# An attention layer with quantised feed-forward: turned rows kept on chip, values moved to the second half, and another order of the weighted sums

## The reference

```python
xn = layernorm(x)                                   # eps 1e-5
q, k, v = (split_heads(xn @ W.T + b) for W, b in ((q_w, q_b), (k_w, k_b), (v_w, v_b)))
attn = softmax(einsum('bhqd,bhkd->bhqk', q / 4, k)) # over all 4096 keys
attention = (attn @ v).reshape(1, 4096, 256) @ out_w.T + out_b
# quant_fp8: scale = min(448 / max|t|, 448), clip(t * scale), round to float8_e4m3
w8, x8 = quant_fp8(weight), quant_fp8(xn)
ffn = bfloat16((x8 @ w8.T) * (x_scale * w_scale) + bias)
out = x + attention + ffn
```

## Time and profile before

| | us |
|---|---|
| median of 3 runs | 1905.43 (1904.55 to 1905.94) |
| profiled execution, its own time | 1905.45 |
| its span | 1903.6 |

### The profile page before, as it was taken

One profiled execution on the slowest core, in us unless ns is written; L12 is line 12 of the kernel. 1 busy time (PEld: TensorE's weight loads), 2 busy tenths in 40 slices (PEclk: granted clock), 3 DMA queues, 4 the chain that ended last, 5 costly groups with the idle time before them and its releaser, 6 DMA issues.

```text
span 1903.6 us, 75615 instructions
## 1 busy us (share of the span) xinstructions
PE 1656.3 (87%) x33482; PEld 564.1 (30%) x33482; DVE 1544.7 (81%) x1974; ACT 1774.4 (93%) x1961; POOL 29.9 (2%) x48
## 2 busy tenths in 40 slices
PE   6978888888888888888888888888888888888888
PEld 4622222222222222222222222222222222222227
DVE  7667888878787887878787887878788887878787
ACT  2359999999999999999999999999999999999991
POOL 0000000000000000000000000000000000000000
PEclk9989999999999999999999999999999999999999
DMA  6640000000010000000010000001000000000002
GB/s 179 205 144 8 23 9 15 21 15 21 7 29 7 16 15 15 21 15 21 7 29 7 11 21 15 21 7 28 7 23 9 15 20 16 21 7 29 7 15 98
DMA packets 62334, 57.12 MB, mean 30 GB/s; under 512 B 20608, under 2 KB 52608, under 8 KB 62016
## 3 DMA queue, kind: packets, MB, share of 16 engines
q1 hardware_dynamic: 62016, 52.36, 9.4%
HBM read 34.74 MB, written 17.30 MB: 27 GB/s over the span
## 4 chain that ended last, share of the span: by engine, by line
ACT 51%; issue 30%; PE 14%; SPq 2%; DVE 1%; ACTq 1%; DMA 0%; DVEq 0%
ACT probs L688 51%; PE banks L1328 5%; PE banks L1297 3%; PE banks L1179 2%; PE banks L1420 1%; PE banks L1190 1%; ACTq L687 1%; DVE o_junk L975 1%; DVE o_sb L974 1%; PE banks L1404 0%; SPq L368 0%; PE banks L1412 0%; PE banks L1163 0%; SPq L371 0%; DMA k_parts<-probs 0%
## 5 line engine op out<-in xcount | busy, mean ns | idle before, releaser
L688 ACT ACTIVATE probs<-banks 128x1024 f32<-128x1024 f32 x1888 | 1731.1, 1193 | 6.7 <-DMA k_parts<-probs 6.2
L1328 PE MATMUL banks<-probs,v_st 64*32 64x512 f32 x15104 | 1004.2, 590 | 2.4
L1297 PE MATMUL banks<-q_st,k_st 50*32 50x512 f16 x16384 | 792.9, 381 | 217.4 <-ACT probs L688 214.2
L1297 PEld LDWEIGHTS banks<-q_st,k_st 50*32 50x32 f16 x16384 | 232.6, 89 | 1151.5 <-ACT probs L688 1093.4
L1008 DVE SCALAR_TENSOR_TENSOR horner<-horner,bits 128x1024 f32<-128x1024 f32 x320 | 393.2, 1229 | 11.0
L1328 PEld LDWEIGHTS banks<-probs,v_st 64*32 64x32 f32 x15104 | 272.0, 106 | 67.4 <-DVE o_junk L975 11.7
L995 DVE TENSOR_SCALAR bits<-banks 128x1024 int32<-128x1024 f32 x160 | 195.9, 1224 | 96.5 <-PE banks L1297 96.5
L1008 DVE SCALAR_TENSOR_TENSOR horner<-bits 128x1024 f32<-128x1024 f32 x160 | 196.1, 1226 | 5.5
L1013 DVE SCALAR_TENSOR_TENSOR d_probs<-horner,powers 128x1024 f32<-128x1024 f32 x160 | 196.0, 1225 | 5.5
L974 DVE COPY o_sb<-banks 128x512 f32<-128x512 f32 x32 | 22.1, 692 | 131.1 <-PE banks L1328 131.1
L1004 DVE TENSOR_SCALAR bits<-bits 128x1024 int32<-128x1024 int32 x160 | 111.1, 695 | 5.5
(11 more groups left out here) (112 smaller groups left out, 465.8 us busy)
## 6 DMA issues: line engine op xcount, KB each, us to landing
q_st<-q_parts SPq DMA_DIRECT2D x204, 32.0 KB, 1.8
k_st<-k_parts SPq DMA_DIRECT2D x102, 64.0 KB, 2.2
k_st<-k_parts SPq DMA_DIRECT2D x102, 60.0 KB, 2.1
q_st<-neg_row SPq DMA_DIRECT2D x264, 1.0 KB, 1.7
xnT_copy<-probs SPq DMA_DIRECT2D x8, 512.0 KB, 3.1
probs<-xnT_copy SPq DMA_DIRECT2D x8, 512.0 KB, 4.3
w_f<-xnT_copy SPq DMA_DIRECT2D x16, 256.0 KB, 2.7
out_dram<-horner SPq DMA_DIRECT2D x16, 256.0 KB, 2.1
```

The source lines that it names most:

```text
L688: act.activation(probs[:, at:at + WIDE * CHUNK].rearrange("p (t c) -> p t c", t=WIDE), banks[:, bank:bank + WIDE, :], ACT.Exp, bias=EXP_SHIFT,
L1297: last = pe.matmul(banks[cols, bank + g, :], k_st[rows, keys], blocks[rows, j], start=True, stop=True, tile_position=(g * GROUP, t * VCOLS))
L1328: last = pe.matmul(banks[VCOLS * qb:VCOLS * (qb + 1), 6 + half, cols], v_st[keys, kt, :], src[keys, g * CHUNK:(g + 1) * CHUNK][:, cols], s ...
```

## The change

- `probs` now holds all eight turned chunks (`xnT`), and they are not loaded again. TensorE turns straight from `xn_all`; POOL's copies are gone.
- All six part buffers lie in `x8T`, the room of the quantised rows.
- In the first pass TensorE does only the first half of q and k; the values stand behind each chunk of the second half. `FIRST_MAX` is 2 in place of 3, and the first maximum uses bank 0 in place of 6.
- SP sets the starting values of semaphores before the load of the values' weights. In the first pass it stores parts only; then it waits for the first pass's parts and loads the whole first head; the turned chunks are stored in the second pass, two with each of its first four chunks.
- ScalarE copies the first turned chunk before it scales the weights, and waits before its first exponential for the eight stores of turned chunks in place of those of parts. VectorE waits for the stores of parts before the first head.
- The planner of the sums: no sum at the place behind one of `takes`; else one at a place unless the place before had one (up to the same backlog rule).
- The two halves of the sampled maximum are two calls, one behind the other.

```diff
-        PART_WORDS = PARTS * CHUNK
-        def as_parts(words):
-
-            return words.bitcast(F16)[:, 0:PARTS * CHUNK].rearrange("p (a c) -> p a c", a=PARTS)
-
-        parts = {2: as_parts(powers), 3: as_parts(bits)}
...
-        xnc = [probs[:, i * CT * D:(i + 1) * CT * D].rearrange("p (t d) -> p t d", t=CT) for i in range(2)]
-        xnTc = [probs[:, (2 + i) * CT * D:(3 + i) * CT * D].rearrange("p (k c) -> p k c", k=KD) for i in range(2)]
-        xnT_again = [probs[:, i * CT * D:(i + 1) * CT * D].rearrange("p (k c) -> p k c", k=KD) for i in range(4)]
-
-        for at, i in enumerate((4, 5, 0, 1)):
-            parts[i] = as_parts(probs[:, 4 * CT * D + at * PART_WORDS:4 * CT * D + (at + 1) * PART_WORDS])
+        xnT_words = KD * CHUNK
+        xnT = [probs[:, n * xnT_words:(n + 1) * xnT_words].rearrange("p (k c) -> p k c", k=KD) for n in range(NCH)]
...
+        part_words = x8T.rearrange("p k s -> p (k s)").bitcast(F16)
+        parts = [part_words[:, i * PARTS * CHUNK:(i + 1) * PARTS * CHUNK].rearrange("p (a c) -> p a c", a=PARTS)
+                 for i in range(6)]
...
-                left = list(range(KT))
+                busy = [p + 1 for p in self.takes]
+                left = [(at, None) for at in range(KT)]
                 self.sums_at = {}
-                p = SUMS_FROM
+                p, resting = SUMS_FROM, False
                 while left:
-                    now = [at for at in left if ready[self.sum_rows[at]] <= p]
-                    take = now[0:1] if (p - SUMS_FROM) % 2 == 0 or len(now) > BACKLOG or p > self.places else []
-                    self.sums_at[p] = [(at, None) for at in take]
+                    now = [piece for piece in left if ready[self.sum_rows[piece[0]]] <= p]
+                    take = [] if p in busy or resting and len(now) <= BACKLOG and p <= self.places else now[0:1]
+                    self.sums_at[p] = take
                     left = left[len(take):]
-                    p += 1
+                    p, resting = p + 1, bool(take)
...
-        FIRST_MAX = 3
+        FIRST_MAX = 2
...
+            def save_xT(n):
+                sp.wait_ge(xT_ready, n * 2 + 2)
+                sp.dma_start(xnT_dram[:, :, n * CHUNK:(n + 1) * CHUNK], xnT[n]).then_inc(xT_saved, 16)
+
+            with sp.Fori(0, NCH // 2) as cc:
                 for par in range(2):
-                    save_chunk(cc, par)
...
+                    save_parts(cc * 2 + par, cc, par, 0)
...
             sp.wait_ge(fills, FILLS)
-            load_k(first, 0, 2)
-            load_k(first, 0, 0)
+            for i in range(4):
+                sp.wait_ge(parts_saved[i], saved_in_half_1(i, 0))
+            load_first_head(first)
             for n in range(NCH):
-                if n + 4 < NCH:
-                    sp.wait_ge(qk_done, 2 * (NCH + n + 1))
-                    load_xT(n + 4)
-                if n == FIRST_MAX + 2:
+                if n == FIRST_MAX + 1:
                     load_rows(first, 0, 1)
+                for kept in range(2 * n, min(2 * n + 2, NCH)):
+                    save_xT(kept)
                 save_parts(n, n // 2, n % 2, 1)
-                if n == 0:
-                    load_q(first, 0, 0)
-                elif n == 1:
-                    load_k(first, 0, 1)
-                elif n == 2:
-                    load_q(first, 0, 1)
+            sp.wait_ge(xT_saved, 16 * NCH)
...
             root(0)
+            copy_turned(0)
             act.wait_ge(scale_ready, 1)
...
-            copy_turned(0, 0, SAVED_0)
             act.wait_ge(scale_ready, 2)
...
-            for i in (4, 5, 0, 1):
-                act.wait_ge(parts_saved[i], saved_in_half_1(i, len(range(i // 2, NCH, 3))))
+            act.wait_ge(xT_saved, 16 * NCH)
...
                 remainders(cc * 2, 0, 0)
-                values(cc * 2)
                 remainders(cc * 2 + 1, 1, 0)
-                values(cc * 2 + 1)
...
+                        values(n)
                         if n < 4:
                             largest_of_x(n)
...
             pe.wait_ge(xn_first, 1)
-            turn_tiles(xn_all)
+            turn_tiles(0)
             pe.wait_ge(q_scaled, 2)
-            pe.wait_ge(w_in["v"], 16)
-            with pe.Fori(0, NCH // 2 - 1) as cc:
-                group(cc, False)
-            group(NCH // 2 - 1, True)
+            for n in range(NCH):
+                pe.wait_ge(xT_ready, n * 2 + 2)
+                project(n, n % 2, 0, xnT[n])
+                if n < NCH - 1:
+                    turn(n + 1)
...
-                            scores(h, n)
+                            if c.order[n % c.places] is None:
+                                for g in range(GROUPS):
+                                    maximum_scores(h, n, g)
+                            else:
+                                scores(h, n)
                             sums_of(h, n)
...
+                    pe.wait_ge(w_in["v"], 16)
                     for n in range(NCH):
-                        pe.wait_ge(xT_back[n % 4], 16 * (n // 4 + 1))
-                        project(NCH + n, n % 2, 1, xnT_again[n % 4])
+                        project(NCH + n, n % 2, 1, xnT[n])
                         if n == FIRST_MAX:
                             pe.wait_ge(c.q_in[0], LOADS)
                             pe.wait_ge(c.k_first, LOADS)
-                            pe.wait_ge(v_done, V_0 + 2 * NCH)
-                            max_part(6, 0, 1).then_inc(c.misc_full, 1)
+                            for g in range(GROUPS):
+                                max_part(0, 0, g, c.misc_full, 1)
+                        project_v(n, n % 2)
```

More of the change, by code:

```diff
@@ L214, in program @@
         amax_shared = sem("amax_shared")
-        xnc_ready = sem("xnc_ready")
         turned = sem("turned")
         xT_ready = sem("xT_ready")
-        xT_saved = [sem(f"xT_saved{i}") for i in range(2)]
-        xT_back = [sem(f"xT_back{i}") for i in range(4)]
+        xT_saved = sem("xT_saved")
         qk_done = sem("qk_done")
@@ L380, in _ @@
             load_x(8, 16, x_in[1])
+            for s, n in ((lo_done, LO_0), (v_done, V_0),
+                         (y_done, 2), (res_done, 2), (out_ready, 2),
+                         (out_saved[0], OUT_0), (out_saved[1], OUT_0)):
+                sp.sem_inc(s, n)
+            for i in range(6):
+                sp.sem_inc(parts_saved[i], SAVED_0)
+            for c in (first, second):
+                sp.sem_inc(c.exp_done, EXP_0)
+                sp.sem_inc(c.pv_done, PV_0)
+                sp.sem_inc(c.acc_free, ACC_0)
+                sp.sem_inc(c.d_taken, D_0)
             load_w("v")
@@ L1190, in project_v @@
                             last = pe.matmul(banks[:, 6 + b, j * D:(j + 1) * D],
-                                             xnTc[par][:, k, t * P:(t + 1) * P], w_sb["v"][:, k, :],
+                                             xnT[n][:, k, t * P:(t + 1) * P], w_sb["v"][:, k, :],
                                              start=(k == 0), stop=(k == KD - 1))
                     last.then_inc(v_mm, 1)
-            def group(cc, last):
-                for par in range(2):
-                    n = cc * 2 + par
-                    pe.wait_ge(xT_ready, n * 2 + 2)
-                    project(n, par, 0, xnTc[par])
-                    if not (last and par):
-                        turn(n + 1, 1 - par)
-                    project_v(n, par)
@@ L1204, in _ @@
             pe.wait_ge(xn_first, 1)
-            turn_tiles(xn_all)
+            turn_tiles(0)
             pe.wait_ge(q_scaled, 2)
-            pe.wait_ge(w_in["v"], 16)
-            with pe.Fori(0, NCH // 2 - 1) as cc:
-                group(cc, False)
-            group(NCH // 2 - 1, True)
-            def attend(c):
-                def max_part(bank, v, halves):
-                    for g in range(GROUPS):
-                        if g:
-                            pe.wait_ge(c.max_half, halves)
-                        rows = slice(g * GROUP, g * GROUP + KROWS)
-                        for j in range(QB // GROUPS):
-                            at, to = v * UG + j * CHUNK, VCOLS * (QB // GROUPS * g + j)
-                            last = pe.matmul(banks[to:to + SAMPLED, bank, :], k_st[rows, 0:SAMPLED], q_st[rows, at:at + CHUNK],
-                                             start=True, stop=True, tile_position=(g * GROUP, to))
-                        if not g:
-                            last.then_inc(c.max_half, 1)
-                    return last
+            for n in range(NCH):
[3 more added lines that the diff above has]
+                    turn(n + 1)
@@ new lines, in attend, with max_part @@
+            def attend(c):
+                def max_part(bank, v, g, done, halves):
+                    if g:
+                        pe.wait_ge(c.max_half, halves)
+                    rows = slice(g * GROUP, g * GROUP + KROWS)
+                    for j in range(QB // GROUPS):
+                        at, to = v * UG + j * CHUNK, VCOLS * (QB // GROUPS * g + j)
```

(3 more changed lines are left out.)

90 lines of the change are left out of this document (23 added, 67 removed).

## The result

| | before | after | ratio (95%) |
|---|---|---|---|
| median of 5 runs each, us | 1905.43 (1903.71 to 1905.94) | 1913.46 (1913.22 to 1914.52) | 1.0044 (1.0033 to 1.0055) |
| profiled execution, its span | 1903.6 | 1911.6 | |
| up to the first exponential | 122.8 | 122.0 | |
| the 1,888 exponentials | 1731.6 | 1740.6 | |
| outputs | 49.2 | 49.0 | |

The account below looks back on a forecast made before the run. ScalarE, busy 93% of the span, was taken to bound the kernel through its 1,888 exponentials. 1905.45 - 0.3 (first piece) + 9.6 (middle piece) = 1914.75, so 1914.8 us; range 1904.5 to 1920.

Parts of the forecast that it names:

- middle piece: The 1731.6 us from first to last exponential, in which ScalarE never stops; forecast to lose 9.6 us.
- first piece: The 122.8 us up to the first exponential; forecast to go to 122.5, -0.3 us, paced by VectorE's row groups.
- The stall at place 19: Sum behind the sampled maximum delays place 20's scores; exponential 0.30 us late in each of 32 units, +9.6 (2.6 to 15.0).
- the rival's condition: At place 19 the sum runs beside the maximum's second half, costing only 2.6 us: 1907.8 in all; chance 0.12.
- Sums at 23, 33, 43 and 53 harmless: Sums at these VectorE places delay the next place's scores no more than before; 0.12 us stays in hand, no loss.
- What is in hand: An exponential's duration less 1.02 us is how early its scores came: 0.20 at place 20, 0.12 at 21.
- the 2.9 that I named as a sign: In the first pass, TensorE idle about 2.9 us per pair of chunks between 25 and 63 us.
- SP's queue: First head's loads, about 18 us from about 71, precede saves; `high` of chunk 3 waits until 95, hidden, costing 0.
- The faster first piece: TensorE, not VectorE's row groups, paces up to the first exponential: 111.3; chance 0.04 with the stall, 0.08 without or small.
- No stall: The changed order of sums does not delay the exponentials at all: 1905.2 us; chance 0.09.
- The longer first piece: Time before the first exponential grows, by slow projection 1 (2.3 us) or late parts (up to 7): 1917 to 1922; chance 0.09.
- the fourth rival: Before projection 1 TensorE idles 2.9 us, the clock halves, costing 2.3; with late parts 1917 to 1922 us; chance 0.09.

Follow-up runs that it names:

- run 1: The changed kernel with the planner of the sums of the kernel before; the first piece stays as changed: 1904.70 us, ratio 0.9998.
- run 2: The kernel before with only the new planner of the sums: 1914.20 us, ratio 1.0045.
- run 3: The changed kernel with its planner also forbidden to put a sum at place 19, the sampled maximum's own: 1913.66 us, ratio 1.0041.
- run 4: The changed kernel with the sum of place 19 put between the two halves of the sampled maximum: 1913.69 us, ratio 1.0045.
- run 7: The kernel of run 1 with ScalarE's square root for the next row group moved behind the two high parts of the even chunk: 1903.01 us, ratio 0.9988.
- run 6: The changed kernel with the old order of sums, values back in the first pass, stores and first head's loads spread, first maximum after chunk 4: 1894.86 us, ratio 0.9950.
- run 5: The changed kernel without the bar on sums at the place behind one of `takes`; the rest after each sum stays: 1904.96 us, ratio 1.0003.

## Why the prediction was right

- **Total.** 1914.8 predicted, 1913.46 measured. The stall in the middle piece and a first piece that hardly changes are both as predicted, and runs 1 and 2 show them apart. Of the 1.3 that it came lower, 0.5 is the first piece (-0.8 for -0.3), 0.6 the middle piece (the single losses of the first unit, which no term held), 0.2 the outputs.
- **The stall at place 19.** Predicted 0.30 for each of 32 units, measured 0.296, at the predicted place and its duration at 1.02. The middle piece was put at 1741.2 (1731.6 + 9.6) and took 1740.6.
- **How it comes about, finer than I had it.** I let the sum start 0.22 behind the maximum's second half. In fact it starts beside it: the second half's two weight loads stand at 192.00, and the sum's view from 191.9 to 192.1 has

```profile
L1265 PE MATMUL banks<-probs,v_st x6: 613/613/613, 192.0 to 192.1; 64*32 64x512 f32 x6
```

six of the first eight matmuls at once; the other two, as many as the tiles that the maximum's second half occupies, come 0.22 later (192.23; that these are the same tiles is an argument, the rows do not name them), and the whole sum takes 1.24 in place of 1.04 from first start to last end. The scores of place 20 show the same lag; they and the end of the sum, in the stretch from 192.7 to 193.3:

```profile
192.23 1.02 PE L1265 MATMUL banks<-probs,v_st 64*32 64x512 f32 x10
192.90 0.58 PE L1224 MATMUL banks<-q_st,k_st 50*32 50x512 f16 x8
```

They take 0.58 from first start to last end where a place's scores take 0.41: six start at 192.90, and the last two at 193.09, 0.86 behind the two late ones of the sum. That is the time at which my working had them, and ScalarE waits for the last. The Trainium skill says that tiles operate independently (TensorEngine Tiling (Array Packing), Key Properties); the trace agrees for the start of the sum. The 2.6 us that I had worked out for this case did not come. So the rival's condition was met in part and its price was wrong; my price was right through the spacing of the row that I took it from, though not every matmul waits that long.
- **Sums at 23, 33, 43 and 53 harmless.** Wrong for 23, and it made no difference here. I had reasoned that the scores of the next place come late by the same amount as behind the places that I looked at, and that TensorE is idle before 23. Runs 3 and 4 show 0.263 at place 24 once place 20 no longer stalls, and no idle time of TensorE from the scores of 21 on; behind 33, 43 and 53 nothing is lost in any run, and the durations at 34, 44 and 54 are 1.14 in the changed kernel, so there the 0.12 stays as predicted. Why 23 and not the others was not tested, nor whether it takes the sum at 21 as well. Place 19 is not ScalarE's, so between the exponentials of 18 and 20, which free the banks for the scores of 21 and 23, lies one step of 0.917 and not two, and TensorE needs 1.3 from the one to the other: that is an argument from the rows.
- **What is in hand.** I took duration less 1.02 for the time by which the scores came early. It is only a lower bound. At place 20 of the kernel before it gives 0.20, but the scores ended at 193.94 (193.53 + 0.41), 0.05 more is the release, and 194.29 would have done: 0.30. At place 22 the scores were done 0.78 before the row of the exponential starts. The forecast was not touched, as it went by 194.29 and not by the duration.
- **The first piece.** Start of projection 0 at 18.9: 18.74. Projection 1 at 28.5: 28.13. A pair of chunks 11.5: 11.32. Last projection at 62.7: 61.79. First exponential at 122.5: 122.0. Of the 0.37 at projection 1 the most is in ScalarE's rows:

```profile
25.84 1.26 ACT L592 ACTIVATE x8T<-banks,qk_bias 128x512 f16<-128x512 f32 x2
26.99 1.08 ACT L584 ACTIVATE probs<-banks 128x512 f32 x2
```

the two high parts begin 0.15 sooner than in the earlier trace rows (25.84 against 25.99), as the row group's data came as much sooner, and the copy follows them after 1.15, not 1.29. TensorE's idle time per pair is 2.18, not the 2.9 that I named as a sign, as a projection and a turn take 9.1 a pair there and not 8.6. What I had wrong beyond that is how much hangs on the row group. I named VectorE's row group as what sets 11.5 against TensorE's 8.6; run 7 shows that the chain through the copy, 5.52 to 5.55 a chunk or 11.07 a pair, was 0.3 behind it.
- **SP's queue.** The first head's loads were to take from about 71 to 89; on the queue they went from 69.42 to 83.6, as the 18 k loads took 8.6 and the 12 q loads 5.5, where the earlier trace rows have 4.68 for six. The wait of `high` is there, 6.4 us until 89.9, and it is hidden as predicted: the projections of the second half follow one another without a gap. The wait for parts before the first exponential is gone.
- **Rivals.** The faster first piece (111.3) did not come, and run 6 shows what it would have needed. No stall: ruled out in the changed kernel, and it is what run 5 has, at 1905.0. The longer first piece did not come in the changed kernel, but it did in two others, below.

## What to carry to other kernels

When one engine is saturated, read for every other engine how late its products come at the tightest place, and count a reordering by the places that it makes later, not by the load that it evens out: here a rule meant to spare the place behind VectorE's made the scores of place 20 some 0.6 us later where 0.3 were in hand, and 0.3 us a unit went straight into the end. The total of the idle column hardly showed this loss (9.4 us where 6.7 had stood, since a wait of 6.2 had gone at the same time, and 0.19 for each 0.30), while the shortest duration and the distance from end to end did. And before work is moved away from an engine that waits for others, ask whether it is what fills the wait: keeping the chunks on chip brought the first exponential 10.9 us forward with the values in the first pass, and 0.8 without them there.

## What the runs showed of the hardware that was not expected

**The clock fell behind 3 us of idle TensorE.** In runs 3 and 4, whose first stage is the changed kernel's own, the profiled execution had a slower projection 1. TensorE's timeline and the windows of run 3 (columns of the earlier trace rows):

```profile
28.59 5.40 PE L1123 MATMUL banks<-probs,d_probs 128*128 128x512 f32 x8 [2.99 <-ACT probs L584]
...
28.00:30.00 2.00, 1.41 (x3) 0.68 (x4) 2.00 (x7) 0.53 (x2) 0.00 (x0) 0.96 0.00 0
30.00:32.00 2.00, 2.00 (x4) 0.87 (x3) 1.49 (x4) 0.69 (x1) 0.00 (x0) 0.50 0.02 8
32.00:34.00 2.00, 2.00 (x6) 0.80 (x5) 0.73 (x1) 0.00 (x0) 0.00 (x0) 0.68 0.84 287
```

The granted clock stood at 0.50, the 1.2 GHz level, from 30 to 32 us, behind 2.99 us without a matmul (3.14 in run 4), and the projection took 5.40 in place of 3.70. It was still at 0.96 from 28 to 30 us, so it fell when the projection had already begun. In the changed kernel, where TensorE had idled 2.19 us, the same stretch is at 1.00:

```profile
30.00:32.00 2.00, 2.00 (x9) 0.99 (x8) 1.69 (x3) 0.76 (x2) 0.00 (x0) 1.00 0.27 96
```

Run 1 had idled 2.54 and run 5 1.39, and their projection 1 took 3.70 too. The first exponential came at 124.2 and 123.9 with the fall, and between 121.7 and 122.1 without. So the fourth rival's mechanism exists, at 1.7 us on the projection where I had put 2.3. How long TensorE idles differs from one execution to the next, with the length of projection 0 (5.36 us in run 4, 6.33 in the changed kernel, with starts 0.2 apart) and with the start of projection 1 (in run 1 it came 0.76 sooner than in run 3, and the clock held although projection 0 took only 5.52). That was only read, not tested. In run 6 the values fill this gap, and its one trace has no such fall.

**A row's duration includes the wait for its turn.** Over the kernels before and after and all seven runs the exponentials' median durations are 1144 to 1190 ns while their pace is 0.917 us, and the four shortest, 1144 to 1147, belong to run 4, the changed kernel and runs 2 and 3, which are the slower ones. A lower median duration in such a group is a sign that the inputs come later, not that the work became cheaper. It is no proof of a loss: run 5 has 1161 against 1187 before and loses nothing. And a row does not include the whole wait: the longest has 1.36, while some scores were done 0.78 before their row starts.
